# Rebuilding the second layer of a two-layer kernel: GELU left in PSUM, attention read from PSUM, own value through a head-summed projection, inverse roots by GpSimd's power operation

## The reference, cut to what matters

```python
xn = _layernorm(x)
# attention over the two sequences as the "seq" axis of length 2, 16 heads in 4 groups, head width 16
qkv = xn @ weight_qkv.T          # per group: 4 queries, 1 key, 1 value
probs = softmax(where(causal, q k^T / sqrt(16), -inf))   # position 0 sees itself, position 1 sees both
s = (probs @ v) @ weight_proj.T
# feed-forward with ternary weights
h = gelu(layer_norm(xn) @ ternary(w_fc).T)               # width 1024
z = layer_norm(h) @ ternary(w_proj).T
x = x + s * silu(z)
```

## Time and profile before

| | |
|---|---|
| median of three runs | 470.88 us (468.42 to 472.22) |
| the profiled execution's own time | 469.96 us |
| its span, first to last instruction | 468.0 us |
| busy share TensorE / VectorE / ScalarE / GpSimd | 75% / 64% / 44% / 57% |
| mean granted TensorE clock | 0.937 |
| layer 1, from GpSimd's first `total` to the end | 305.36 to 468.0 us |

### The profile page before, as it was taken

One profiled execution on the slowest core, in us unless ns is written; L12 is line 12 of the kernel. 1 busy time (PEld: TensorE's weight loads), 2 busy tenths in 40 slices (PEclk: granted clock), 3 DMA queues, 4 the chain that ended last, 5 costly groups with the idle time before them and its releaser, 6 DMA issues.

```text
span 468.0 us, 6901 instructions
## 1 busy us (share of the span) xinstructions
PE 352.9 (75%) x2114; PEld 272.6 (58%) x2114; DVE 298.4 (64%) x864; ACT 204.5 (44%) x483; POOL 266.5 (57%) x272
## 2 busy tenths in 40 slices
PE   0999878687989687897998898106577767676774
PEld 0884345475877566686776777105366556565663
DVE  4929993555654253455666474246979778788766
ACT  1344242633443234643444453013563754745781
POOL 6440004177878667778888787472865566352550
PEclk9999997999999899998999999856999799799999
DMA  8760036968788798776877755490000000000000
GB/s 275 280 201 0 1 103 202 301 160 215 185 180 194 200 255 199 181 180 140 196 169 188 178 96 70 76 327 4 0 22 1 23 2 24 23 1 23 24 22 22
DMA packets 37558, 57.86 MB, mean 124 GB/s; under 512 B 6075, under 2 KB 27155, under 8 KB 37139
## 3 DMA queue, kind: packets, MB, share of 16 engines
q1 hardware_dynamic: 25235, 38.55, 25.5%
q0 software_dynamic: 12288, 18.88, 22.0%
HBM read 39.69 MB, written 17.73 MB: 123 GB/s over the span
## 4 chain that ended last, share of the span: by engine, by line
DVE 29%; PE 24%; DMA 13%; issue 12%; ACT 11%; POOL 10%; SPq 0%; ACTq 0%; POOLq 0%; DVEq 0%
DMA acc_d<-W,idxE 8%; POOL acc_d L457 5%; ACT W L704 3%; DMA W<-tok_d,idxE 3%; POOL W L437 3%; PE two L1320 3%; PE two L1368 3%; PE two L1284 3%; ACT A L720 2%; PE two L1193 2%; DVE F L1113 2%; DVE A L1107 2%; PE two L1380 2%; DVE ni L1054 1%; DMA x<-in_q 1%
## 5 line engine op out<-in xcount | busy, mean ns | idle before, releaser
L457 POOL DMA_INDIRECT acc_d<-W,idxE x64 | 102.4, 1599 | 30.7 <-issue 13.0
L437 POOL DMA_INDIRECT W<-tok_d,idxE x56 | 56.7, 1012 | 62.5 <-DMA tok_d<-F 45.7
L1019 DVE SCALAR_TENSOR_TENSOR W<-W,two 128x88 f32<-128x88 f32 x64 | 15.6, 244 | 63.8 <-ACT W L648 62.0
L632 ACT ACTIVATE W<-two 128x256 f32<-128x256 f32 x64 | 24.4, 381 | 51.7 <-PE two L1357 51.1
L1487 PE MATMUL two<-W,A 128*128 128x257 f16 x256 | 34.3, 294 | 16.6 <-DVE A L1107 16.6
L1487 PEld LDWEIGHTS two<-W,A 128*128 128x128 f16 x256 | 26.0, 105 | 25.0 <-issue 20.2
L1107 DVE TENSOR_TENSOR A<-W,A 128x1024 f16<-128x1024 f32 x16 | 26.7, 1670 | 21.4 <-ACT A L720 21.4
L1320 PE MATMUL two<-A,v 128*128 128x128 f32 x256 | 33.1, 284 | 6.7 <-issue 6.7
L1454 PE MATMUL two<-F,wfcT 128*128 128x256 f16 x256 | 31.0, 277 | 9.3 <-ACT W L704 9.3
L1320 PEld LDWEIGHTS two<-A,v 128*128 128x128 f32 x256 | 32.0, 199 | 8.9 <-issue 8.4
L1357 PE MATMUL two<-ident,W 128*128 128x128 f32 x112 | 22.8, 286 | 14.9 <-DMA W<-tok_d,idxE 12.7
(11 more groups left out here) (217 smaller groups left out, 884.6 us busy)
## 6 DMA issues: line engine op xcount, KB each, us to landing
W<-in_gu SPq DMA_DIRECT2D x20, 352.0 KB
F<-in_gu SPq DMA_DIRECT2D x12, 352.0 KB
acc_d<-xn SPq DMA_DIRECT2D x8, 512.0 KB, 4.2
W<-in_dn SPq DMA_DIRECT2D x20, 176.0 KB
F<-in_dn SPq DMA_DIRECT2D x12, 176.0 KB
x<-in_q SPq DMA_DIRECT2D x4, 512.0 KB, 7.1
A<-in_Wo SPq DMA_DIRECT2D x1, 2048.0 KB, 13.0
tok_d<-xn SPq DMA_DIRECT2D x4, 512.0 KB, 4.3
```

Of the source, the lines that this page charges most:

```text
L437: pool.indirect_dma_start(out=xg[n % XR], out_offset=None, in_=tok_d[:, :], in_offset=bass.IndirectOffsetOnAxis(ap=idxE[:, n:n + 1], axis=0))\
L457: pool.indirect_dma_start(out=acc_d[n % 2][:, :], out_offset=bass.IndirectOffsetOnAxis(ap=idxE[:, n:n + 1], axis=0), in_=ysb[n % YS], in_o ...
L632: sc.activation(xgT[n % 2], bk_(2)[:, 0:D].rearrange("p (k n) -> p k n", k=KH), ACT.Copy)\
```

## The change

- GELU writes back to the PSUM bank it read. Each chunk of 128x512 is then read there by `high`, `square` (ScalarE) and `low` (VectorE), so that halves of 1024 become chunks of 512, and a bank is free only after the chunk's `low`.
- `fc` is issued chunk by chunk between other TensorE work, `down1` chunk by chunk.
- `sum_squares` is one reduction of 2048 elements with a stride.
- q is not copied out of PSUM. The score scale goes into the weights, the token's scale into the tanh. `products` on VectorE takes the place of `score_products` on GpSimd. GpSimd keeps one multiplication, `weigh`.
- The own values and their sum with the new ones go through one transpose and a projection whose rows are summed over the four heads (`wpoS`, made from a new input `wpo4`, 512 KB). The transposes are three for four; the projection's matmuls are four as before.
- `take_s1` goes: `attended` on VectorE multiplies straight from PSUM. `finish` loses its multiplication.
- GpSimd makes the inverse roots with one `pow` of at most 128x6; one Newton round of three steps remains on VectorE.
- `gated` multiplies s0 by the expert total ahead of the gate. The queues have a new order.

In the diff the conditions on p inside the three long loops (first ScalarE, then VectorE, then TensorE) are left out.

```diff
+            def gated(p):
+                pool.wait_ge(s0_ready, 2 * p + 2)
+                pool.wait_ge(acc_ready, p + 1)
+                pool.tensor_tensor(pair(s0, p), pair(s0, p), pair(xn, p), ALU.mult).then_inc(gated_ready, 1)
             def add_gated(p):
                 pool.wait_ge(silu_ready, p + 1)
-                pool.wait_ge(s0_ready, 2 * p + 2)
-                then(pool.tensor_tensor(tg[p % 2], tg[p % 2], pair(s0, p), ALU.mult))
                 pool.tensor_tensor(pair(x, p), pair(x, p), tg[p % 2], ALU.add).then_inc(x1_ready, 1)
+            def weigh(p):
+                pool.wait_ge(td_ready, p + 1)
+                if p:
+                    pool.wait_ge(attT_ps, p)
+                pool.tensor_tensor(tdv.rearrange("p (g r d) -> p g r d", r=REP1, d=HD1), heads(dkv[:, :, HD1:2 * HD1]),
+                                   td[:, :].rearrange("p (g r) -> p g r", r=REP1).unsqueeze(3)
+                                   .to_broadcast([P, NKV1, REP1, HD1]), ALU.mult).then_inc(tdv_ready, 1)
+            def roots(p):
+                c = root_cols(p)
+                pool.wait_ge(v_in, p + 3)
+                pool.tensor_tensor(ny[:, c], nv[:, c], expo[:, c], ALU.pow).then_inc(root_ready, 1)
+            for p in range(-AHEAD, NP):
+                if p >= 0:
+                    weigh(p)
+                if p + AHEAD < NP:
+                    total(p + AHEAD)
+                    gated(p + AHEAD)
+                if p >= -2:
+                    roots(p)
+                if p + AHEAD < NP:
+                    add_gated(p + AHEAD)
+                if 0 <= p < LAST:
+                    finish(p)
...
+                sc.activation(fc_bank(n), fc_bank(n), ACT.Gelu, scale=gwv[:, 0:1]).then_inc(gelu_ready, 1)
+                sc.wait_ge(gelu_ready, n + 1)
+                sc.activation(hiT[p % 2][:, 512 * j:512 * j + 512], fc_bank(FC * p + j), ACT.Copy).then_inc(hi_ready, 1)
+                sc.activation(sq[:, 512 * j:512 * j + 512], fc_bank(FC * p + j), ACT.Square).then_inc(sq_ready, 1)
...
+            for p in range(-AHEAD, NP):
+                    high_x(p + 1)
+                    half_tanh(p)
+                    hidden(p + 1, 0)
+                    hidden(p + 1, 1)
+                    take_attT(p)
+                    gate(p + AHEAD)
+                    take_kv(p + 1)
+                    gate2(p)
+                    hidden(p + 1, 2)
+                    hidden(p + 1, 3)
...
+                last = mark(ve.scalar_tensor_tensor(out=dkv, in0=new[:, :, REP1 * HD1:GS1], scalar=scale, in1=kv0[p % 2],
+                                                    op0=ALU.mult, op1=ALU.subtract))
+                ve.scalar_tensor_tensor(out=own[p % 2][:, 1], in0=new[:, :, GS1 - HD1:GS1], scalar=scale,
+                                        in1=own[p % 2][:, 0], op0=ALU.mult, op1=ALU.add).then_inc(own_ready, 1)
+                ve.wait_ge(dve, last)
+                ve.tensor_tensor(pr, new[:, :, 0:REP1 * HD1].rearrange("p g (r d) -> p g r d", r=REP1),
+                                 heads(dkv[:, :, 0:HD1]), ALU.mult).then_inc(prod_ready, 1)
...
+                ve.tensor_tensor(loT[p % 2][:, cols], fc_bank(n), hiT[p % 2][:, cols], ALU.subtract).then_inc(lo_ready, 1)
...
+                ve.tensor_reduce(sq1, sq.rearrange("p (c t) -> p t c", t=PW), AX.X, ALU.add).then_inc(sqsum_ready, 1)
...
+                for q_ in range(GT):
+                    ve.scalar_tensor_tensor(out=zu[:, q_, :], in0=bk_(6)[:, D * q_:D * q_ + D],
+                                            scalar=zhalf[p % 2][:, q_:q_ + 1], in1=zu[:, q_, :], op0=ALU.mult, op1=ALU.mult)\
+                        .then_inc(s1_used, 1)
...
+            for p in range(-AHEAD, NP):
+                    low_x(p + 1)
+                    sum_squares(p)
+                    moments(p + 2)
+                    spreads(p)
+                    low(p + 1, 0)
+                    newton(p)
+                    half_scale(p)
+                    normalise(p + 2)
+                    products(p + 1)
+                    low(p + 1, 1)
+                    score_difference(p + 1)
+                    silu2(p)
+                    silu(p + AHEAD)
+                    low(p + 1, 2)
+                    attended(p)
+                    low(p + 1, 3)
...
+            for p in range(-1, NP):
+                    turn_x(p + 1)
+                    for j in range(FC):
+                        down1(p, j)
+                    fc(p + 1, 0)
+                    fc(p + 1, 1)
+                    turn_att(p)
+                    square_sums(p)
+                    qkv(p + 1)
+                    fc(p + 1, 2)
+                    fc(p + 1, 3)
+                    project(p)
...
+                    for cols, scale in QKV_PARTS:
+                        sc.activation(q_cols(wqT_hi, cols), q_cols(wqkv_s, cols), ACT.Copy, scale=scale).then_inc(wq_hi_ready, 1)
+                    sc.activation(wpoT[:, :, :], wpoT[:, :, :], ACT.Copy, scale=0.5).then_inc(wpo_ready, 1)
...
+                ve.tensor_reduce(wpoS[0][0:KV1, :], by_head[0:KV1], AX.X, ALU.add).then_inc(wpo_ready, 1)
+                then(ve.tensor_reduce(wpoS[1][KV1:2 * KV1, :], by_head[KV1:2 * KV1], AX.X, ALU.add))
```

More of the change, by code:

```diff
@@ L108, in build @@
         wpoT = sb("wpoT", [P, KH, D])
+        wpoS = [sb(f"wpoS{i}", [P, D]) for i in range(2)]
         WoS = sb("WoS", [P, D])
@@ L723, in own_value, with hidden @@
[L723 to L727 removed]
+                sc.activation(sq[:, 512 * j:512 * j + 512], fc_bank(FC * p + j), ACT.Square).then_inc(sq_ready, 1)
+            def hidden(p, j):
+                if p < NP:
+                    gelu(p, j)
+                    high(p, j)
+                    square(p, j)
             def half_tanh(p):
@@ L1078, in moments @@
                 mark(ve.tensor_scalar(nv[:, 0:GT], var, EPS_LN, None, ALU.add))
-                then(ve.tensor_scalar(nv[:, GT:2 * GT], var, 1.0 + EPS_Q, EPS_Q * EPS_LN, ALU.mult, ALU.add))
+                ve.wait_ge(dve, step[0])
+                ins = ve.tensor_scalar(nv[:, GT:2 * GT], var, 1.0 + EPS_Q, EPS_Q * EPS_LN, ALU.mult, ALU.add)
+                if p < 2:
+                    ins.then_inc(v_in, 1)
+                    ve.wait_ge(v_in, p + 1)
+                else:
+                    then(ins)
             def normalise(p):
@@ L1155, in _ @@
             centre_weights()
-            silu(0)
-            silu(1)
-            for p in range(2):
-                moments(p)
-                newton(slice(0, 2 * GT))
-                normalise(p)
-                if p == 0:
-                    silu(2)
-                    low_x(0)
-            score_difference(0)
-            low(0, 0)
-            for p in range(NP):
-                low(p, 1)
-                if p + 2 < NP:
-                    moments(p + 2)
-                sum_squares(p)
-                if p + 1 < NP:
-                    low_x(p + 1)
-                if p + 3 < NP:
-                    silu(p + 3)
-                spreads(p)
-                newton(slice(0, 3 * GT) if p + 2 < NP else slice(2 * GT, 3 * GT))
-                half_scale(p)
-                if p + 2 < NP:
+            for p in range(-AHEAD, NP):
+                if 0 <= p + 1 < NP:
+                    low_x(p + 1)
+                if p >= 0:
+                    sum_squares(p)
+                if 0 <= p + 2 < NP:
+                    moments(p + 2)
+                if p >= 0:
+                    spreads(p)
+                if 0 <= p + 1 < NP:
+                    low(p + 1, 0)
+                if p >= -2:
+                    newton(p)
+                if p >= 0:
+                    half_scale(p)
+                if 0 <= p + 2 < NP:
                     normalise(p + 2)
-                silu2(p)
-                if p + 1 < NP:
+                if 0 <= p + 1 < NP:
+                    products(p + 1)
+                    low(p + 1, 1)
                     score_difference(p + 1)
-                    low(p + 1, 0)
+                if p >= 0:
+                    silu2(p)
+                if p + AHEAD < NP:
+                    silu(p + AHEAD)
+                if 0 <= p + 1 < NP:
+                    low(p + 1, 2)
+                if p >= 0:
+                    attended(p)
+                if 0 <= p + 1 < NP:
+                    low(p + 1, 3)
             close()
```

346 lines of the change are left out of this document (143 added, 203 removed).

## The result

| | before | after |
|---|---|---|
| median | 471.26 us (468.42 to 472.22, 4 runs) | 444.49 us (440.70 to 447.38, 4 runs) |
| span of the profiled execution | 468.0 us | 445.6 us |
| its own time | 469.96 us | 447.38 us |
| layer 1, from the first `total` to the end | 162.6 us | 133.4 us |
| mean granted clock | 0.937 | 0.932 |

The ratio is 0.941, 95% interval 0.935 to 0.947. The forecast was 429.0 us with a range of 420 to 443: the gain is real, 27 us, but 15.5 us smaller than forecast, and the median is 1.5 us outside the range. Lines L...

The account below looks back on a forecast made before the run. VectorE's queue was taken as the bound: 12.27 us, 12.6 per period with the exposed power pass. Layer 0's end, head, pairs and tail gave 424.7, plus 1.96 outside the span 426.7, plus 2.4 for clock: 429 us, range 420 to 443.

Parts of the forecast that it names:

- its clock term: Whole kernel: one stretch of TensorE at half clock, as in every other earlier period, costs some 2.4 us.
- Layer 0's end: End of layer 0: 305.4 us plus 1.0 for longer constants, head sums mostly hidden behind scatters, and the `wpo4` load.
- the price of `sum_squares`: VectorE's reduction of 2048 elements per pair: 2.30 us if the stride costs nothing, upper bound 4.5.
- rival 3: The strided reduction costs double, 2.2 us more in each of eight pairs: 446 us; chance 0.08.
- The power pass: GpSimd's `pow` of six columns per pair: 0.8 us, of which 0.3 exposed on VectorE with hand-over, period 12.6 us.
- rival 4: Slower than before, `pow` running element by element: gain used up at 4.8 us a pass, 520 at 10; chance 0.07.
- The rest of the queue: VectorE's other steps per period, such as `low`, `moments`, Newton, `products`, within a queue summed to 12.27 us.
- The stalls: VectorE standing still behind GpSimd, about 2 us of each earlier period; small steps were to take 0.16 to 0.20 us.
- Rival 2: Stalls move to `moments`, `normalise` and `silu` beside GpSimd's `gated` and `add_gated`: 1.2 us per period return, 438 us; chance 0.08.
- rival 1: TensorE becomes the bound if the clock stays at 0.82: period 14.5 us, 440 us; chance 0.17.
- The tail and the head: Layer 1's two ends: head 22.2 us to the last `low`, tail from `sum_squares` to the span's end about 9.9.
- Pair 6: Last pair of layer 1, without `moments`, `normalise` and `silu`, but waiting for `take_kv` and following ScalarE: 11.2 us.

Follow-up runs that it names:

- experiment 2: Changed kernel with the sum-of-squares reduction reading eight neighbours, without the stride (it adds up wrong elements): 434.90 us, ratio 0.920.
- experiment 6: Changed kernel with GpSimd's power pass undone, seed and three Newton rounds on VectorE as before: 453.73 us, ratio 0.965.
- experiment 7: Changed kernel with GELU writing to SBUF, where `high`, `square` and `low` read it: 450.11 us, ratio 0.958.
- experiment 8: Changed kernel with two more GpSimd additions of 128x512, whose result nothing reads, behind each pair's power pass: 461.89 us, ratio 0.982.
- 9: Changed kernel with the strided reduction replaced by the earlier kernel's tree of three contiguous additions: 444.04 us, ratio 0.939.
- experiment 10: Changed kernel with the sum of squares moved from VectorE to TensorE, sixteen one-column f16 matmuls per pair: 429.74 us, ratio 0.910.
- 12: On top of experiment 11: head sums made after layer 0, and layer 1's first power pass issued ahead of GpSimd's product for pair 1: 427.76 us, ratio 0.908.
- experiment 3: Changed kernel with the two head sums moved from layer 0's expert loop to after `centre_weights`, `wpo4` loaded later: 442.91 us, ratio 0.937.
- experiment 11: On top of experiment 10: the power pass issued in two parts, four columns and then two: 428.26 us, ratio 0.911.
- experiment 5: Changed kernel with ScalarE writing the squares in turned order, so the reduction reads eight neighbours, result correct: 441.38 us, ratio 0.935.

## Why the prediction was off

The sum was 426.7 us without its clock term; the median is 444.5. By the layer-1 span the forecast had 22.2 + 75.0 + 11.2 + 9.9 = 118.3 us, and 133.4 were measured: 15.1 us too little. Layer 0's end was put 2.7 us too early, and the 2.4 us for a stretch at half clock never came. 15.1 + 2.7 - 2.4 = 15.4 us is the miss.

- **The failed step is the price of `sum_squares`**, "2.30 for 2048, if the stride costs nothing". The mechanism, VectorE's queue as the bound, was right; this term of its sum was not. The arithmetic fits a flat reduction (2.28 us, 2.19 to the next step, measured in experiment 2), but the operation is strided, and 3.61 us is what it costs: 1.31 us in each of eight pairs, 10.5 us, and 10.8 by experiment 2. The upper bound of 4.5 us had been set down, with rival 3 at 0.08 for its full price; the value in between was given no weight of its own. Between 2.30 and 4.5 no row lay nearer to one end, and the range stopped at 443. Two thirds of the miss are this term.
- **The power pass**: taken at 0.8 us between 0.10 and 1.27, measured 1.33 for six columns, 1.02 for four, 0.71 for two. VectorE waits 0.72 us in each of six pairs, and by the prediction's own count, from the end of `low`'s 0.60, it is 0.81 us instead of 0.3: 3.1 us. In pair 6 there is no such wait; the passes in head and tail add part of a microsecond each. So this term too was mis-sized, and it is the second largest part. It came out above the upper end of the bracket. As rival 4 (element by element at 4.8 us and more) it did not occur, and experiment 6 shows it is worth its place.
- **The rest of the queue** came out as summed: 14.38 = 12.57 + 1.31 + 0.51, less 0.01. `low` 0.60, `silu2` and `attended` 0.66 and 0.78, `products` 0.78 for 0.85, Newton 0.60. For the 65 ns that the Trainium skill, "VectorE: DVE Perf Modes", section "The TRN2 errata", gives a PSUM source on top, there was no place in the rows of before, and there is none in after: 0.69 us for `low` from PSUM here and 0.69 for `low` from SBUF in experiment 7, where nothing holds it up.
- **The stalls** went as forecast, but partly for a reason that the prediction did not see, and that part is luck. It said that the long steps read PSUM, and experiment 7 shows what that is worth for `low`. But the small steps are spared because GpSimd's instructions happen to stand beside the one long reduction with a single input; experiments 8, 9 and 10 bring the stalls back by changing what stands beside what. Rival 2 was a real danger. The rule that the prediction quoted from the Trainium skill ("SBUF — State Buffer", section "Who interferes with whom") holds in these runs too, and experiment 8 shows it: 1.23 for 0.17 us beside a 1.27 us addition.
- **TensorE** (rival 1) did not become the bound: clock 1.00 and 11.80 us busy, close to the 12.1 computed. Before, periods at 0.82 and at 1.00 took turns; in after all six full periods are at 1.00. What made the difference was not tried apart.
- **The tail and the head**: the tail took 12.0 us for 9.9. Its terms in the prediction add up to 10.1; the reduction with `square_sums` took 4.4 us for 2.9, and each of the other three terms 0.1 to 0.2 more than forecast. Pair 6 took 12.2 for 11.2, where the reduction alone adds 1.3; the head took 23.6 for 22.2, with the first `pow` at 1.05 us for 0.8. Issuing that pass ahead of GpSimd's product (12) only moved a stall.
- **Layer 0**: the forecast had its end at 305.4 + 1.0 = 306.4, and by medians it is 309.1: 1.3 us since the profiled execution of before was an early one (306.7 by medians), and 1.4 more than the 1.0 allowed. The head sums with their small step took 4.1 us for the 2.8 forecast. That they hide behind the scatters, as the prediction said, is not borne out: the scatters wait some 2 us less where the sums are late (experiment 3), though the medians don't show it in full. How the 1.4 us divide is open: the 512 KB load and the longer constants were not tried apart.

## What to carry to other kernels

Price a reduction by how it steps through memory, not by its number of elements: if the trace holds no strided row, give the stride a range of its own and let the forecast's range take in its middle. When an engine's small steps stand still behind a neighbour, look at which instructions stand beside which before and after a change: shortening or replacing the one that happened to cover them brings the stall back, and a forecast of the gain must subtract it (3.61 us removed, 2.0 gained). An experiment has to be checked for having moved what it was to move, as experiment 11 did not. And an engine that does not set the pace may be the cheapest adder: sixteen one-column f16 matmuls took no more of TensorE (0.39 us) than the four f32 matmuls they replaced (0.46).

## What the runs showed of the hardware

- A VectorE reduction of 2048 f32 to 256 takes 3.69 us when its eight elements lie 1 KB apart and 2.28 us when they are neighbours, both with GpSimd's additions beside it; of 1024 on 64 partitions to 256, with the four 1 KB apart, 1.88 us, against 1.22 us for the flat one of the earlier trace rows.
- A ScalarE square that writes turned, each element 32 bytes from the next, takes 1.10 us for 512 elements instead of 0.59 (experiment 5).
- GpSimd's power pass takes 0.71, 1.02 and 1.33 us for 2, 4 and 6 columns, some 0.16 us per column above 0.4 us, where its addition of 512 elements per partition takes 1.27.
- GpSimd and VectorE hold each other up in both directions where VectorE has two SBUF inputs (experiments 7 and 9): a VectorE addition of 256 elements 1.37 for 0.43 us, a GpSimd one 1.60 for 0.62, a power pass 1.84 for 1.33. Also a small VectorE instruction with one SBUF input can be held up (TENSOR_SCALAR, 1.00 for 0.17 us, experiment 10).
- ScalarE writes GELU into PSUM no slower than into SBUF: 0.67 us against 0.68 in experiment 7 and 0.69 in the earlier trace rows.
- Layer 0's end moved between 305.4 and 312.3 us from one profiled execution to the next, also of the same kernel (307.94 and 312.23).
